# Attention scores of a talking-heads layer as two 64-row matmuls side by side, with mixed queries exchanged between partition halves

## The reference

```python
q, k, v = heads(x @ Wqkv.T + bqkv)            # 16 heads of 16
q, k = rope(q), rope(k)
logits = einsum('bhid,bhjd->bhij', q, k) * SCALE
logits = einsum('bhij,gh->bgij', logits, Wpre)     # heads mixed before
attn = softmax(logits)
attn = einsum('bhij,gh->bgij', attn, Wpost)        # and after
out = einsum('bhij,bhjd->bhid', attn, v)
x = layernorm(x + out @ Wout.T + bout)
xn = layernorm(x) * gamma + beta
logits = l2norm(xn) * scale @ l2norm(mu)           # 256 expert slots
slot_in = softmax(logits over rows).T @ xn
h = gelu(slot_in @ w1 + b1);  slot_out = h @ w2 + b2
out = softmax(logits over slots) @ slot_out
x = layernorm(x + out)
```

## Time and profile before

| what | value |
|---|---|
| time, median of 3 executions | 8595.84 us |
| lowest and highest | 8595.69 and 8598.14 us |
| the profiled execution, first to last instruction | 8594.9 us |
| mean granted TensorE clock | 0.984 of full speed |
| busy: TensorE, VectorE, ScalarE, POOL | 97%, 89%, 84%, 78% |
| matmuls | 158060 |

### The profile page before, as it was taken

One profiled execution on the slowest core, in us unless ns is written; L12 is line 12 of the kernel. 1 busy time (PEld: TensorE's weight loads), 2 busy tenths in 40 slices (PEclk: granted clock), 3 DMA queues, 4 the chain that ended last, 5 costly groups with the idle time before them and its releaser, 6 DMA issues.

```text
span 8594.9 us, 399875 instructions
## 1 busy us (share of the span) xinstructions
PE 8315.6 (97%) x158060; PEld 4655.0 (54%) x158060; DVE 7684.5 (89%) x11341; ACT 7251.8 (84%) x13696; POOL 6719.8 (78%) x14053
## 2 busy tenths in 40 slices
PE   8999999998999999999899999999989999999997
PEld 4555555555455555555545555555554555555554
DVE  7999999997899999999789999999978999999996
ACT  6898989896689898989569899898957989898895
POOL 7788888884788888888478888888847888888883
PEclk9999999998999999999899999999989999999998
DMA  0000000002000000000200000000020000000002
GB/s 32 7 7 9 8 8 9 9 8 76 18 6 7 9 8 9 7 9 8 76 18 6 8 9 8 9 7 9 8 76 18 6 8 9 9 8 8 9 8 81
DMA packets 98674, 141.23 MB, mean 16 GB/s; under 512 B 7840, under 2 KB 88352, under 8 KB 94496
## 3 DMA queue, kind: packets, MB, share of 16 engines
q1 hardware_dynamic: 96800, 115.48, 4.0%
HBM read 73.51 MB, written 39.85 MB: 13 GB/s over the span
## 4 chain that ended last, share of the span: by engine, by line
PE 73%; DVE 10%; issue 9%; POOL 4%; ACT 2%; DVEq 0%; POOLq 0%; ACTq 0%
PE psS L1193 47%; PE psP L1213 15%; PE psO L1228 6%; DVE big L848 3%; DVE pl L876 3%; DVE top L839 2%; PE psM L1239 1%; ACT big L676 1%; DVE ot L859 1%; PE psS L1359 1%; PE psS L1330 1%; POOL pl L524 1%; PE psM L1254 1%; POOL at L452 0%; PE psS L1165 0%
## 5 line engine op out<-in xcount | busy, mean ns | idle before, releaser
L848 DVE SCALAR_TENSOR_TENSOR big<-psP,big 128x512 f16<-128x512 f32 x4096 | 2623.2, 682 | 303.7 <-ACT big L676 266.6
L676 ACT ACTIVATE big<-psP 128x512 f16<-128x512 f32 x4096 | 2199.0, 588 | 646.0 <-PE psP L1213 646.0
L839 DVE TENSOR_REDUCE top<-psS 128x1 f32<-128x1024 f32 x2048 | 2491.8, 1217 | 246.8 <-PE psS L1193 246.5
L1193 PE MATMUL psS<-KH,AH 128*128 128x512 f16 x8192 | 2465.7, 383 | 64.3 <-POOL AL L465 41.7
L1193 PE MATMUL psS<-KH,AL 128*128 128x512 f16 x8192 | 2441.9, 380 | 0.0
L1193 PE MATMUL psS<-KL,AH 128*128 128x512 f16 x8192 | 2441.0, 380 | 0.0
L657 ACT ACTIVATE pr<-psS,nb 128x1024 f32<-128x1024 f32 x2048 | 2283.9, 1115 | 67.8 <-POOL pl L524 1.4
L686 ACT ACTIVATE ph<-pr 128x1024 f16<-128x1024 f32 x2048 | 2165.3, 1057 | 64.7
L876 DVE TENSOR_TENSOR pl<-pr,ph 128x1024 f16<-128x1024 f32 (+1 forms) x2048 | 2149.0, 1049 | 1.3 <-issue 1.2
L1213 PEld LDWEIGHTS psP<-rh,ph 64*128 64x128 f16 x32768 | 1434.1, 95 | 857.2 <-DVE big L848 488.7
L1213 PE MATMUL psP<-rh,ph 64*128 64x64 f16 x32768 | 1681.9, 192 | 62.4 <-DVE big L848 54.0
(11 more groups left out here) (136 smaller groups left out, 7489.1 us busy)
## 6 DMA issues: line engine op xcount, KB each, us to landing
ph<-in_xT SPq DMA_DIRECT2D x16, 512.0 KB, 7.8
xr<-in_x SPq DMA_DIRECT2D x64, 128.0 KB, 2.1
Q<-in_w SPq DMA_DIRECT2D x8, 1024.0 KB, 7.3
out<-V SPq DMA_DIRECT2D x16, 512.0 KB, 3.8
d_x<-x SPq DMA_DIRECT2D x60, 128.0 KB, 2.0
d_xn<-xn SPq DMA_DIRECT2D x60, 128.0 KB, 2.3
d_lg<-lg SPq DMA_DIRECT2D x60, 128.0 KB, 2.0
d_ct<-cT SPq DMA_DIRECT2D x60, 128.0 KB, 1.7
```

Of the source, the lines that this page charges most:

```text
L676: a.activation(PT[:, hf * JH:(hf + 1) * JH, :, 0, i0:i0 + HQ], psP[:, ih, :].rearrange("p (j g i) -> p j g i", j=JH, g=H), ACT.Copy, scale ...
L839: v.tensor_reduce(top[:, t % 2, h:h + 1], psS[:, 2 * h:2 * h + 2, :].rearrange("p c n -> p (c n)"), X, ALU.max).then_inc(s_mx, 1)
L848: v.scalar_tensor_tensor(out=PT[:, js, :, 1, i0:i0 + HQ], in0=psP[:, ih, :].rearrange("p (j g i) -> p j g i", j=JH, g=H), scalar=MDROP, in ...
L1193: mm = pe.matmul(psS[:, c, :], A_[:, k8, k, :], K_[:, k, c * CW:(c + 1) * CW], start=n == 0, stop=n == 5)
```

## The change

The contraction of 256 features is cut into 4 quarters (`KQ`) of 64 rows instead of 2 tiles of 128. The keys of the even chunk of a pair lie on partitions 0 to 63, those of the odd chunk on 64 to 127, each with all 4 quarters (`KH`, `KL`: partitions x 4 x 2 pairs x 512; the same size as before). The mixed query must then be there for both halves of the partitions. POOL writes it as before into two of the four quarters of `AX`, and for each slot SP sends two DMAs of 64 partitions x 1 KB that copy each half's quarters to the other half (`exchange`); one semaphore per buffer (`s_ax`) tells the scores. `AX` has twice the size of `AH` and `AL` together.

`scores` now handles a pair of chunks: 12 steps of two matmuls, one for each half of the array's rows, into the two banks of the pair, 48 a slot instead of 24. `pieces` 0 and 1 stand together behind the first pair, 2 and 3 behind the second. The row load and the stores are put between the exchanges of fixed slots. In the projections the keys come as two tiles of 64 columns from two chunks at once, which changes the order of TensorE, VectorE and the loads of chunks 2 and 3, and needs the rope tables once more in a layout by halves (`cosk`, `sink`, in the memory of `AX`), four more table DMAs a batch.

```diff
-        KH = sb("KH", [P, KT, N], F16)
-        KL = sb("KL", [P, KT, N], F16)
+        KH = sb("KH", [P, KQ, NP, CW], F16)
+        KL = sb("KL", [P, KQ, NP, CW], F16)
...
-        AH = sb("AH", [P, TG, KT, P], F16)
-        AL = sb("AL", [P, TG, KT, P], F16)
+        AX = sb("AX", [P, TG, KQ, 2, P], F16)
...
+                for half in range(2):
+                    rows = slice(half * HP, (half + 1) * HP)
+                    for dst, src in ((cosk, cos_t), (sink, sin_t)):
+                        by_pair = src[rows, :].rearrange("p (c two n) -> p c two n", c=NP, two=2)
+                        sp.dma_start(dst[rows, :, :], by_pair[:, :, half, :]).then_inc(s_w, 16)
...
-                for c in range(2, NC):
-                    sp.wait_ge(s_v, b * (NC * 2) + 2 * (c - 1))
-                    keys_load(b, c)
+                sp.wait_ge(s_k, b * (2 * NC) + 4)
+                keys_load(b, 2)
+                sp.wait_ge(s_v, b * (2 * NC) + 4)
+                keys_load(b, 3)
...
+                def exchange(it, t):
+
+                    T = (b * NIT + it) * TI + t
+                    k8 = t % TG
+                    sp.wait_ge(s_A, T * 4 + 4 + 1)
+                    for half in range(2):
+                        mine, other = slice(half * HP, (half + 1) * HP), slice((1 - half) * HP, (2 - half) * HP)
+                        sp.dma_start(AX[mine, k8, KT:KQ, :, :], AX[other, k8, 0:KT, :, :]).then_inc(s_ax[k8], 16)
+
                 row_load(0)
-                with sp.Fori(0, NIT - 1) as r:
-                    row_load(r + 1)
-                    row_stores(r)
+                for t in range(LEAD):
+                    exchange(0, t)
+                for it in range(NIT):
+                    for t in range(TI):
+                        if it < NIT - 1 or t + LEAD < TI:
+                            exchange(it + (t + LEAD) // TI, (t + LEAD) % TI)
+                        if t == 3 and it >= 1:
+                            row_load(it)
+                        for r, at in in_work(it):
+                            if t - 1 == at.get("norm"):
+                                store_normed(r)
+                            if t - 1 == at.get("turn_c"):
+                                store_routed(r)
+                store_routed(NIT - 2)
...
-                    g.tensor_copy(AH[:, t % TG, :, :], at[:, :, :]).then_inc(s_A, 1)
+                    g.tensor_copy(AX[:, t % TG, 0:KT, 0, :], at[:, :, :]).then_inc(s_A, 1)
...
+                def keys(c):
+
+                    part = c % 2
+                    for half in range(2):
+                        pe.wait_ge(s_xT[half], b * (8 * NC) + 16 * (c // 2) + 16)
+                    for f in range(2):
+                        if c >= 1:
+                            pe.wait_ge(s_kp, b * (4 * NC) + 4 * (c - 1) + 2 * f + 2)
+                        for k in range(KT):
+                            for half in range(2):
+                                w0 = (2 + f) * P + (half ^ part) * HP
+                                mm = pe.matmul(psS[half * HP:(half + 1) * HP, 2 + f, :], wqk_s[:, k, w0:w0 + HP],
+                                               xT_s[half][:, k, :], start=k == 0, stop=k == KT - 1,
+                                               tile_position=(0, half * HP))
+                        mm.then_inc(s_k, 1)
...
+                for c in range(NC):
+                    for work in ((queries, values, keys), (keys, queries, values))[c % 2]:
+                        work(c)
...
-                def scores(T, t, c, fresh):
+                def scores(T, it, t, hp, fresh):
 
                     k8 = t % TG
-                    if c == 0:
-                        pe.wait_ge(s_A, T * 4 + 4 + 1)
-
+                    if hp == 0:
+                        pe.wait_ge(s_ax[k8], ((b * NIT + it) * 2 + t // TG) * 32 + 32)
                     if not fresh:
-                        pe.wait_ge(s_exp, (T - 1) * 2 + c // 2 + 1 + 1)
-                    n = 0
-                    for A_, K_ in ((AH, KH), (AL, KH), (AH, KL)):
-                        for k in range(KT):
-                            mm = pe.matmul(psS[:, c, :], A_[:, k8, k, :], K_[:, k, c * CW:(c + 1) * CW],
-                                           start=n == 0, stop=n == 5)
-                            n += 1
+                        pe.wait_ge(s_exp, (T - 1) * 2 + hp + 1 + 1)
+                    steps = [(s_, K_, kq) for s_, K_ in ((0, KH), (1, KH), (0, KL)) for kq in range(KQ)]
+                    for n, (s_, K_, kq) in enumerate(steps):
+                        for half in range(2):
+                            rows = slice(half * HP, (half + 1) * HP)
+                            mm = pe.matmul(psS[:, 2 * hp + half, :], AX[rows, k8, kq, s_, :], K_[rows, kq, hp, :],
+                                           start=n == 0, stop=n == len(steps) - 1, tile_position=(half * HP, 0))
                     mm.then_inc(s_S, 1)
...
                     if live:
-                        scores(T, t, 0, first and t < 1)
-                    pieces(0)
-                    if live:
-                        scores(T, t, 1, first and t < 1)
-                    pieces(1)
+                        scores(T, it, t, 0, first and t < 1)
+                    pieces(0, 1)
```

More of the change, by code:

```diff
@@ L48 @@
 CW = N // NC
+NP = NC // 2
+KQ = 2 * KT
 JC = JT // NC
@@ L187, in seq_layer @@
         wv_s = plf[:, KT * 4 * P:KT * (4 * P + DIM)].rearrange("p (k f) -> p k f", k=KT)
+        axf = AX[:, :, :, :, :].rearrange("p t q s n -> p (t q s n)").bitcast(F32)
+        cosk, sink = (axf[:, i * NP * CW:(i + 1) * NP * CW].rearrange("p (c n) -> p c n", c=NP) for i in range(2))
         xT_s = [phf[:, i * KT * CW:(i + 1) * KT * CW].rearrange("p (k n) -> p k n", k=KT) for i in range(2)]
@@ L237, in seq_layer @@
         s_A = sem("s_A")
+        s_ax = [sem(f"s_ax{k}") for k in range(TG)]
         s_S = sem("s_S")
@@ L400, in _ @@
                 sp.dma_start(CT[:, last, :], cT[:, :, :].rearrange("p k n -> p (k n)")).then_inc(s_st, 16)
+                sp.wait_ge(s_S, tiles * 2)
                 tables()
@@ L804, in _ @@
                 for c in range(NC):
-                    n_ = slice(c * CW, (c + 1) * CW)
-                    v.wait_ge(s_w, b * 64 + 64)
+                    v.wait_ge(s_w, b * NW_DMA + NW_DMA)
                     base = b * (4 * NC) + 4 * c
[L809 to L825, removed]
+                    part, pair = c % 2, c // 2
@@ new lines, in _, with rope @@
+                    b0, b1_ = bqk_s[:, 2 + 2 * part:3 + 2 * part], bqk_s[:, 3 + 2 * part:4 + 2 * part]
+                    def rope():
+                        for f, (q0, q1), bias in ((0, (kc0, ks0), b0), (1, (ks1, kc1), b1_)):
+                            v.wait_ge(s_k, b * (2 * NC) + 2 * c + f + 1)
+                            for dst, tab in (((q0, cosk), (q1, sink)), ((q0, sink), (q1, cosk)))[f]:
+                                v.scalar_tensor_tensor(out=dst, in0=psS[:, 2 + f, :], scalar=bias, in1=tab[:, pair, :],
+                                                       op0=ALU.add, op1=ALU.mult).then_inc(s_kp, 1)
+                        v.wait_ge(s_kp, base + 4)
+                        v.tensor_tensor(kr0, kc0, ks1, ALU.subtract).then_inc(s_rk, 1)
+                        v.tensor_tensor(kr1, ks0, kc1, ALU.add).then_inc(s_rk, 1)
@@ new lines, in v_bias @@
+                    def v_bias():
+                        for h in range(2):
+                            n_v = b * (2 * NC) + 2 * c + h
+                            v.wait_ge(s_v, n_v + 1)
+                            if c >= 1:
+                                v.wait_ge(s_vl, n_v - 1)
+                            v.tensor_tensor(vb[h].rearrange("p j g d -> p j (g d)"),
+                                            psP[:, h, :].rearrange("p (j d) -> p j d", j=2),
+                                            bv_s[:, :].unsqueeze(1).broadcast_to([P, 2, DIM]),
+                                            ALU.add).then_inc(s_vc, 1)
@@ L826, in _ @@
+                    for work in ((v_bias, rope), (rope, v_bias))[part]:
+                        work()
                     for k, kr in enumerate((kr0, kr1)):
                         v.wait_ge(s_kh, b * (2 * NC) + 2 * c + k + 1)
-                        v.scalar_tensor_tensor(out=KL[:, k, n_], in0=kr, scalar=KSCALE, in1=KH[:, k, n_],
+                        v.scalar_tensor_tensor(out=KL[:, part * KT + k, pair, :], in0=kr, scalar=KSCALE,
+                                               in1=KH[:, part * KT + k, pair, :],
@@ L1153, in _, with queries @@
             with pe.Fori(0, B) as b:
-                pe.wait_ge(s_w, b * 64 + 64)
-                for c in range(NC):
+                pe.wait_ge(s_w, b * NW_DMA + NW_DMA)
+                def keys(c):
[3 more added lines that the diff above has]
+                    for f in range(2):
+                        if c >= 1:
+                            pe.wait_ge(s_kp, b * (4 * NC) + 4 * (c - 1) + 2 * f + 2)
```

(7 more changed lines are left out.)

32 lines of the change are left out of this document (20 added, 12 removed).

## The result

The changed kernel takes 8614.85 us (median), the kernel before in the same comparison 8597.68 us: a ratio of 1.0022 (95% interval 1.0014 to 1.0030). It is slower by 0.2%, where 8345 us had been forecast. Its profiled execution spans 8618.9 us.

A forecast was written before the change was run, and what follows sets the result against it. TensorE, busy 97% of the span, was taken to bound the kernel, with ScalarE and VectorE close behind in the slots. Span 8594.9 - 262 (slots) + 8 (exchange) + 4 (table loads) = 8345 us; range 8220 to 8490.

The forecast's parts named there:

- (a): Scores in the attention slots: 12 pairs of 64-row, 512-column matmuls a half slot, 216 ns each, 2.59 us.
- Rival 3: Slower: 512-column score pairs don't quite run together; 8820 us at 240 ns, about 13,540 one after the other; chance 0.10.
- (b): TensorE's form switches in 16 slots: 5.3 + 1.4 - 0.8 = 5.9 us saved, so TensorE needs 118.2 us.
- (c): Waits in 16 slots: ScalarE adds 1.5 us, VectorE 0.3, present waits 0.3; 120.3 us, saving 262 us over 64 turns.
- the waits of before: The 0.3 us in 16 slots in which TensorE already waits, kept in the forecast.
- Rival 2: The ring of three engines gives nearly nothing in plain slots; 128 us saved elsewhere, 8480 us; chance 0.18.
- (d): Exchange DMAs in the slots: hidden, except 2 us before each batch's first scores, 8 us in all.
- (e): Projections: extra table loads hidden except before batch 0, 4 us; changed order of loads and queries, 0 a batch.
- The landing: Wait for the exchange's transfer before a batch's first scores: 2 us, x 4 = 8 us.
- the start: Extra table loads before batch 0, not hidden behind the expert layer: 4 us.

The follow-up runs named there:

- both cuts: Changed kernel with ScalarE's high part and VectorE's low part each cut by 256 columns a half: 8333.3 us; kernel before with the same cuts: 8554.0 us.
- split: Changed kernel with the output pieces back inside the scores (6 pairs, a piece, 6 pairs, a piece, turn): 8571.4 us, 0.9975 of the kernel before.
- split3: Changed kernel with the output pieces after the fourth and eighth of the 12 score pairs: 8590.1 us, 0.9999 of the kernel before.

## Why the prediction was wrong

**(a), array work: right.** The pair of 512 columns costs the 216 ns that the turn row suggested. Rival 3 fell, and with it an efficiency below 2, as it might have been read out of the 3.07 for four row tiles of 512 columns in the Trainium skill ("TensorE: Matmul & The Clock Gate", section "Measured speedup vs the span model"): 12 pairs of row tiles took 2.59 us here, the time of 12 single matmuls. The about 4 ns for each further tile in the same section of the Trainium skill don't appear in that stream either.

**(b), switches: right.** Last scores to turn went from 0.31 to 0.21 us and turn to scores from 0.12 to 0.03, the `psM` groups pay twice as foreseen. With the waits removed (both cuts) 16 slots take 119.8 us in the mean, of which some 2 are gaps inside blocks; 118.2 was the estimate of the work.

**(b) again, what it left out: wrong by 2.0 us in 16 slots.** Putting two output pieces together was counted as a saving of 1.4 us and nothing else. This is the first step that failed. In fact it made TensorE run through 352 instructions at 7 ns each, faster than they came. Gaps inside blocks grew by 1.1 us (turn), 0.3 (output) and 0.5 (scores) in 16 slots, 2.0 x 64 = about 125 us. The trace of before had only a weak sign, 8 us of such gaps, but it had the rate: a weight load and a matmul each 14 ns in the turn. I read the pair spacing there and did not ask where the instructions came from.

**(c), what is late next: right engines, wrong size and place.** This is the second step that failed. I gave ScalarE 1.5 us, VectorE 0.3 and the waits of before 0.3 in 16 slots. Measured: between last scores and turn TensorE spends 10.13 us in 16 slots, and 6.12 with the waits gone, so 4.0 and not 2.1. And it doesn't wait where I put it, at the scores for `pr`, but at the turn for `mixed_low`. My slot-by-slot account took one ring (exponential to scores) and let the output slots refill it. The other ring (turn, ScalarE's `mixed_high`, VectorE's `mixed_low`, next turn) has less slack, and behind VectorE's output copy it makes slot 4 longer than before (9.53 against 9.10 us; I had 8.7). By stretches: the two output slots took 23.1 us against my 21.2, slots 3 to 9, of which I wrote that TensorE sets them, 51.8 against 50.0, and slots 11 to 1 49.2 against 48.4. Rival 2, "nearly nothing in plain slots", describes the 14 slots without output: 101.8 us before, 101.0 after. It had a chance of 0.18 and a price of 8480, since it kept the 1.4 us of the output slots, which the gaps had turned into a loss (22.7 to 23.1 us for both).

**(d) and (e), edges: too small.** 12 us were forecast, 44 came. The landing was right (2.6 us a batch; from the last projection to the first scores 8 us in all), and so was the start (5.3 us against 4). The projections, which (e) put at 0, took 2.1 to 2.9 us more in each batch, 10 us in all, and without the exchange still 7. The last turns took 2 us more. The expert layer took 9, with the scatter named above; that part is open. And the final output of a batch, 256 matmuls in a row, takes 8.25 us instead of 6.13 (batch 0), 10 us in the four batches. Here is the one of batch 1, before and after (timeline of TensorE):

```profile
4225.93 3.93 PE L1228 MATMUL psO<-big,V 128*32 128x128 f16 x161
4231.03 1.52 PE L1228 MATMUL psO<-big,V 128*32 128x128 f16 x95 [1.17 <-issue]
```
```profile
4236.66 3.13 PE L1295 MATMUL psO<-big,V 128*32 128x128 f16 x120
4241.21 1.98 PE L1295 MATMUL psO<-big,V 128*32 128x128 f16 x127 [1.42 <-issue]
4245.04 0.33 PE L1295 MATMUL psO<-big,V 128*32 128x128 f16 x9 [1.85 <-issue]
```

The matmuls and their order are the same in both kernels. Before, one packet border falls into them, behind the 161st in all four batches; after the change two do, 127 matmuls with their weight loads apart, again in all four. So part of what the instruction supply costs is where the borders happen to fall.

The sum by the corrected terms: 5.9 saved, less 2.0 of gaps, less 3.7 of new waits, is 0.2 us in 16 slots (0.3 measured), 13 to 20 us in all; less 44 at the edges is 24 us slower by the spans, which is what the spans show (8594.9 and 8618.9).

## What to carry to other kernels

When one engine is busy 99.7% and two others 90 to 93% of a stage, their idle time says little of what a faster first engine brings: cut the work of the others for a test run first, one and then both, and see whether the saving has anywhere to go. Follow every ring of waits that passes through the engine, not the most obvious one. And count instructions as well as columns: short matmuls in long unbroken runs can outrun their own instruction stream, and the same work with something slower in between can be faster, if no other engine's wait takes the gain (`split` gained, `split3` did not).

## What the runs showed of the hardware

Two half-array streams of 512 columns into two banks run side by side at the rate of one (12 pairs in 2.59 us). TensorE's instruction supply ran dry at about 14 ns for each weight load and matmul together. The gaps stood at packet borders, 256 instructions or a multiple of it apart (109 of 113); in the inner turns of the changed kernel they were 0.5 to 1.9 us long and ended 1.2 to 1.6 us behind the landing of a 16 KB packet (all 74 in scores and turns). A change between 128x128 tiles and tiles of 64 rows cost 0.10 us one way and 0.09 back (last scores to turn 0.31 us before and 0.21 after, turn to scores 0.12 and 0.03). 2048 transfers of 64 KB between partition halves, 128 KB in each slot, had no effect on the stage that could be seen.
